# Plain fp32 products beside the transpositions, their remainders later on VectorE, and one GpSimd multiply ahead of a normalization, in a fused decoder layer

## What is computed

```python
q  = x + x @ Wq + bq;  ks = x + x @ Wk[k] + bk[k];  vs = x + x @ Wv[k] + bv[k]     # k = 0, 1
states = einsum('kbhnd,kbhne->kbhde', ks / 32, vs / 32)                            # per head, 16 x 16
state  = states[0] * states[1]
x1 = layernorm(x + (layernorm(q @ state) * ln_g + ln_b) @ Wo + bo)
sim  = (x1 @ Wqx.T) . (ctx @ Wk.T) * 64 ** -0.5                                    # 16 heads, 64 keys
attn = softmax(sim);  x2 = layernorm(x1 + (attn . (ctx @ Wv.T)) @ Wout.T + b_out)
```

## Time and profile before

| | |
|---|---|
| median of 3 runs | 1239.56 us (1238.46 to 1239.6) |
| the profiled execution | 1244.09 us, span 1242.4 us |
| mean granted TensorE clock | 0.99 of full speed |
| busy over the span | PE 97%, PE weight loads 85%, VectorE 69%, GpSimd 47%, ScalarE 45% |
| one iteration of the attention | about 48.5 us, 16 of them from about 112 us to 890 us |

### The profile page before, as it was taken

One profiled execution on the slowest core, in us unless ns is written; L12 is line 12 of the kernel. 1 busy time (PEld: TensorE's weight loads), 2 busy tenths in 40 slices (PEclk: granted clock), 3 DMA queues, 4 the chain that ended last, 5 costly groups with the idle time before them and its releaser, 6 DMA issues.

```text
span 1242.4 us, 27256 instructions
## 1 busy us (share of the span) xinstructions
PE 1203.1 (97%) x10512; PEld 1051.2 (85%) x10512; DVE 863.1 (69%) x1694; ACT 555.1 (45%) x1097; POOL 585.8 (47%) x968
## 2 busy tenths in 40 slices
PE   8987999999999999999999999989999999999998
PEld 7866888888888888888888888877799899899888
DVE  5545988889889889889898898988523423432435
ACT  2124556555555555465555555545523412421420
POOL 2223665666666666656666565655322112202201
PEclk9988999999999999999999999999999999999999
DMA  9821011021111011110211111310211022021001
GB/s 274 222 65 35 12 59 54 26 60 45 35 52 53 26 61 36 43 61 19 61 44 36 52 53 35 115 50 26 95 69 69 1 69 69 1 69 69 1 1 35
DMA packets 88739, 70.07 MB, mean 56 GB/s; under 512 B 41378, under 2 KB 82083, under 8 KB 88612
## 3 DMA queue, kind: packets, MB, share of 16 engines
q1 hardware_dynamic: 86580, 67.67, 18.0%
q10 hardware_dynamic: 2032, 0.66, 0.2%
HBM read 42.09 MB, written 26.22 MB: 55 GB/s over the span
## 4 chain that ended last, share of the span: by engine, by line
PE 71%; DVE 8%; issue 7%; POOL 6%; ACT 1%; POOLq 0%; DVEq 0%
PE sim L137 6%; PE sim L138 6%; PE sim L139 6%; PE ob L137 5%; PE ob L138 5%; PE ob L139 5%; PE pt L497 4%; PE pw L391 3%; PE pt L139 2%; PE pt L138 2%; PE pt L137 2%; PE pw L137 2%; PE pw L454 2%; PE pw L138 2%; PE pw L139 2%
## 5 line engine op out<-in xcount | busy, mean ns | idle before, releaser
L1619 POOL TENSOR_TENSOR w_lo<-w_raw,w_hi 128x2048 fp32r<-128x2048 f32 x16 | 73.8, 4614 | 220.9 <-ACT w_hi L1559 167.8
L137 PE MATMUL ob<-b_hi,pT_hi 128*128 128x256 f32 x512 | 151.0, 295 | 0.5 <-DVE pT_lo L879 0.5
L138 PE MATMUL ob<-b_lo,pT_hi 128*128 128x256 f32 x512 | 143.6, 280 | 0.0
L139 PE MATMUL ob<-b_hi,pT_lo 128*128 128x256 f32 x512 | 143.6, 280 | 0.0
L968 POOL TENSOR_TENSOR prob<-prob,rz 128x512 f32<-128x512 f32 x128 | 131.1, 1046 | 12.6 <-DVE rz L816 12.6
L732 ACT ACTIVATE pT_hi<-pt 128x512 fp32r<-128x512 f32 x128 | 76.2, 595 | 111.2 <-PE pt L497 110.6
L726 ACT ACTIVATE prob<-prob 128x512 f32<-128x512 f32 x128 | 81.1, 633 | 99.1 <-DVE prob L872 99.0
L137 PEld LDWEIGHTS ob<-b_hi,pT_hi 128*128 128x128 f32 x512 | 96.9, 189 | 9.0 <-issue 5.4
L138 PEld LDWEIGHTS ob<-b_lo,pT_hi 128*128 128x128 f32 x512 | 97.1, 190 | 1.9
L139 PEld LDWEIGHTS ob<-b_hi,pT_lo 128*128 128x128 f32 x512 | 96.3, 188 | 0.0
L867 DVE TENSOR_REDUCE mx<-sim 128x8 f32<-128x512 f32 x128 | 87.8, 686 | 6.6 <-PE sim L139 4.4
(11 more groups left out here) (244 smaller groups left out, 3726.5 us busy)
## 6 DMA issues: line engine op xcount, KB each, us to landing
xraw<-in_x SPq DMA_DIRECT2D x16, 512.0 KB, 4.0
kv_scratch<-stage SPq DMA_DIRECT2D x32, 256.0 KB, 3.6
x_scratch<-x SPq DMA_DIRECT2D x64, 128.0 KB, 1.7
out_x<-o_sb SPq DMA_DIRECT2D x64, 128.0 KB, 1.7
w_raw<-in_L_ffn_experts_inter SPq DMA_DIRECT2D x8, 1024.0 KB, 5.1
w_raw<-in_L_ffn_experts_out SPq DMA_DIRECT2D x8, 1024.0 KB, 7.8
kraw<-kv_scratch SPq DMA_DIRECT2D x16, 256.0 KB, 2.9
vraw<-kv_scratch SPq DMA_DIRECT2D x16, 256.0 KB, 2.8
```

The lines of the kernel that those rows point to most:

```text
L137: pe.matmul(out, lh, rh, start=first, stop=False)
L138: pe.matmul(out, lh, rl, start=False, stop=False)
L139: return pe.matmul(out, ll, rh, start=False, stop=last)
```

## The change

Three kinds of edit:

- `ORDER`: `B0`/`B1` move on TensorE from between the halves of `ob` in slot 0 to the end of the slot, in front of the next slot's transposes, on ScalarE to the start of slot 1 and on VectorE behind the sum and statistics there. `B2`/`B3` move in slot 1 from between the score halves to behind them, in front of the second transposes, with ScalarE and VectorE following later in the slot (VectorE behind the second shift). `A1`/`A3` move in slot 2 from between the halves of `ob` to the end of the slot; ScalarE and VectorE do them in slot 3, VectorE one at the very start and one behind the sum and statistics. `ST` moves in slot 3 on TensorE behind the second score half, and on VectorE from behind the first shift to behind the second.
- `pool_p`: the multiply of one half of the probabilities by `rz` becomes a function.
- `pool_slot`: in slot 2 the multiply of the first half stands ahead of `rstd` of the first norm; in all other slots the order stays.

```diff
     ORDER = {
-        "B0": ((0, 7), (0, 8), (1, 0)), "B1": ((0, 7), (0, 8), (1, 0)),
-        "B2": ((1, 1), (1, 1), (1, 3)), "B3": ((1, 1), (1, 1), (1, 3)),
+        "B0": ((0, 8), (1, 0), (1, 1)), "B1": ((0, 8), (1, 0), (1, 1)),
+        "B2": ((1, 2), (1, 3), (1, 5)), "B3": ((1, 2), (1, 3), (1, 5)),
...
-        "A1": ((2, 7), (2, 8), (2, 10)), "A3": ((2, 7), (2, 8), (2, 10)),
-        "ST": ((3, 1), (3, 1), (3, 3)),
+        "A1": ((2, 8), (3, 0), (3, 0)), "A3": ((2, 8), (3, 0), (3, 1)),
+        "ST": ((3, 2), (3, 1), (3, 5)),
...
+    def pool_p(pool, q, h):
+
+        part = by_head(prob[:, q, h * HK:(h + 1) * HK])
+        pool.tensor_tensor(part, part, rz[:, q, h * 8:h * 8 + 8].unsqueeze(2).broadcast_to([P, 8, NKV]),
+                           ALU.mult).then_inc(s["p_ready"], 1)
+
...
+        if has_sim and slot == 2:
+            need(pool, "rz_made", n + 1)
+            pool_p(pool, q, 0)
         if has_z and it != -1:
             pool_rstd(pool, 0, n + 4, q)
         if has_sim:
             need(pool, "rz_made", n + 1)
-            for h in range(2):
-                part = by_head(prob[:, q, h * HK:(h + 1) * HK])
-                pool.tensor_tensor(part, part, rz[:, q, h * 8:h * 8 + 8].unsqueeze(2).broadcast_to([P, 8, NKV]),
-                                   ALU.mult).then_inc(s["p_ready"], 1)
+            if slot != 2:
+                pool_p(pool, q, 0)
+            pool_p(pool, q, 1)
         if has_z and it != -1:
             pool_rstd(pool, 1, n + 4, q)
```

## The result

The changed kernel takes 1267.48 us (median of 4 runs, 1265.22 to 1268.38) against 1239.58 us (4 runs), a ratio of 1.0218 with a 95% interval of 1.0205 to 1.0231: slower by 27.9 us. 1266.6 us was forecast. Its profiled execution has a span of 1265.2 us.

The account below looks back on a forecast made before the run. Slot 3 was taken as bound by a chain from ST through GpSimd, ScalarE and VectorE to the queries. 14 iterations x 1.9 = 26.6 us, +0.5 without ST, -0.1 last batch: +27.0, so 1239.6 becomes 1266.6, range 1257 to 1280.

Parts of the forecast that it names:

- TensorE's switches: Each moved block saves about 0.05 us on TensorE; B0/B1 and B2/B3 together 0.10 an iteration, A1/A3 and ST where TensorE waits.
- The B remainders: In slot 1 on ScalarE and VectorE, the same operations in another order, costed at nothing; at most 1.2 us.
- GpSimd's multiply and rstd: Slot 2: first multiply 1.3 us sooner, TensorE's 0.45 wait gone; rstd ends near 534.8 instead of 534.3, VectorE idle some 0.9.
- VectorE's order: Slots 2 and 3: pT_lo 0.6 us later, ST 1.9 later behind the second shift; VectorE's own work reaches zw_lo unchanged.
- What queues behind it: Slot 3: GpSimd's state, nmr, ScalarE's norms, zw_hi, zw_lo and the queries all come 1.9 us later behind the late ST.
- TensorE's two waits: Slot 3: TensorE stands about 1.2 us before SB and 1.5 (elsewhere 1.7) before the queries.
- The rule by occupancy: A skill rule to optimize the busiest engine: TensorE's savings alone would count and time would fall; slot 3 speaks against it.
- The last but one iteration: The iteration without ST: VectorE's +0.6 us meets a bound softmax chain, forecast to cost +0.5 us.
- the last one: The last batch's iteration: the B moves were forecast to gain 0.1 us.
- The clock: Rival, 9%: slot 3's new waits lower the granted clock, up to 22 us more, 1289; in a third of iterations 1274.
- The second rival: 5%: TensorE's stream decides, sprod reached by 540.2 as before, 0.65 us gained an iteration, about -9 us, 1230.
- The third, no change: 3%: VectorE's own work reaches zw_lo at the same time and ScalarE's norms do not wait for nmr: 1239 us.

Follow-up runs that it names:

- only_b: The kernel before with only the ORDER rows of B0 to B3 from the change: 1237.56 us, iterations of 48.46 us, ratio 0.9979.
- only_pool: The kernel before with only GpSimd's first multiply of slot 2 put ahead of rstd: 1240.1 us, iterations of 48.54 us, ratio 1.0006.
- state_late: The changed kernel with GpSimd's state multiplies called in slot 3 behind the last norm's factors and the x1 bias: 1243.39 us, ratio 1.0025.
- st_early: The changed kernel with ST's operations on VectorE back behind the first shift: 1250.42 us, iterations of 49.16 us, ratio 1.0078.
- only_state_late: The kernel before with only GpSimd's state multiplies called in slot 3 behind the last norm's factors: 1240.55 us, ratio 1.0003.
- only_st: The kernel before with only ST's row of the change: 1260.97 us, iterations of 49.84 us, ratio 1.0176.
- state_late_old_rstd: As state_late, with GpSimd's rstd ahead of the first multiply in slot 2 again: 1237.94 us, iterations of 48.35 us, ratio 0.9975.
- state_late_a_undone: The changed kernel with A1/A3 as before and GpSimd's state multiplies moved as in state_late: 1232.41 us, iterations of 48.09 us, ratio 0.9945.
- state_late_only_b: As state_late_a_undone, but with ST's row as in the kernel before: 1236.3 us, iterations of 48.45 us, ratio 0.9983.

## Why the prediction was right

**TensorE's switches.** Right: `B0`/`B1` and `B2`/`B3` save 0.09 an iteration together (`only_b`), 0.10 was taken. The B remainders were costed at nothing, and nothing shows, as `only_b` has the whole gain. What a switch is made of stays open: the products of L454 and L443 run on quarters of the array (64*64 in their rows), so the kind of operand and the tiling change together. From a transposition to fp32r products, both on the whole array, the first step of `sim` takes 0.32 us instead of 0.23 (544.78 to 545.10, then 545.33), so part of the price needs no change of tiling. The 0.05 taken for `A1`/`A3` and for `ST` was not measured alone.

**GpSimd's multiply and rstd.** Right in both directions. The first multiply starts 0.09 us behind the end of `rz`, the transposition of slot 3 no longer waits, and VectorE stands 1.03 us for `rstd`, where 0.9 was reckoned. Alone, the reordering is worth nothing (`only_pool`).

**VectorE's order.** `pT_lo` was to come 0.6 later and `ST` 1.9. Counted from the start of slot 2, `pT_lo` comes at 13.76 instead of 13.07, 0.7 later, which is 0.6 with the slot's earlier start of nearly 0.1; `ST` 2.04, or 1.96. VectorE's own work was to reach `zw_lo` where it did: it is through 1.80 us before 556.66, at 545.2 on the old time axis, against 545.14.

**What queues behind it.** The step on which all hung. `state_late` takes nothing away but this queue, and `st_early` nothing but the maximum and shift in front of `ST`; they return 24 and 17 of the 28 us, and VectorE's amount of work, the same in all three, cannot explain either. The prediction gives TensorE's two waits as about 1.2 us, and 1.7 in its rivals or 1.5 among its signs; they are 0.96 and 1.40 of idle time, or 1.1 and 1.55 by the distance of the starts less the 0.12 of a matmul. On the old time axis the state was to be ready at 543.3 and the queries at 547.5; both hold within 0.1.

**The rule by occupancy.** The Trainium skill, Perfetto Trace Analysis, section Identifying the Most-Contended Engine, would have picked TensorE here too. Over the whole it is the busiest, but the change shortened slots 0 to 2 by 0.6 us together (34.75 us against 35.36) and the time rose; so the trace disagrees with reading the sum from TensorE's share. The Trainium skill, Perfetto Trace Analysis, section Optimization Strategy, says to find the gaps on that engine and the semaphore that each waits for. The trace agrees with this one: the two gaps of slot 3, now 0.96 and 1.40 us, name the chain.

**The sum.** Thirteen whole iterations grew by 1.91 us each, 24.8 together, and the three slots of the first one that are seen behind its start by 2.1: 26.9 us, where 26.6 was forecast for fourteen. Behind them two small terms were mis-sized. The last but one iteration, which has no `ST`, was underrated: its slots 2 and 3 take 22.49 us in `st_early`, which has the same order there, against 21.55 before, +0.94 instead of +0.5. In the last one the gain was underrated: its four slots take 39.83 us instead of 40.54, 0.7 less, where the B moves were given 0.1; `only_b` has the same shorter slot 1 (9.66 instead of 10.61) and longer slot 2 (11.05 instead of 10.72). That the two errors nearly cancel is luck. In the profiled execution of the change a fall of the clock, shown in the last section, adds another 1.56 us in slot 2 of the last but one iteration. With 0.07 saved in that iteration's first two slots, all that makes 28.6 us from slot 1 of the first batch to the end of the last slot (779.26 us against 750.65), and 27.1 without that fall, where 27.0 was forecast. The spans differ by only 22.8, because the setup took 5.8 us less in the one execution than in the other, and the medians by 27.9, which carry that scatter too.

**The rivals.** The clock did not fall inside the iterations: the granted clock is 1.00 in all four slots, and 1.00 from 140 to 809 us, in spite of the two waits. The second rival, a gain, asked for `sprod` by 540.2; on the old time axis it came at 542.1. The third, no change, asked that ScalarE's norms did not wait for `nmr`; they waited 3.05 us. `state_late` is the change with that condition made true, and it is 0.23 us an iteration over the kernel before, which is TensorE's wait in front of `SB`, less what it gains elsewhere.

## What to carry to other kernels

A wait belongs to the instruction's engine, not to the work it is for: before moving a producer later, look at which engine waits for it and list everything that stands behind that wait in its program. Here four operations of 0.7 us moved by 1.3 us held up a norm, a split and the queries on three other engines. Where two chains arrive at the same place together, shortening one alone gives nothing (`only_state_late`, 0.00 us), and lengthening it costs nearly in full (`only_st`, 1.29 of 1.33). Here a gain beyond the 0.09 of `B0` to `B3` came only when GpSimd's queue was out of the way and `ST` came late on VectorE, where it fills a wait: 48.35 in `state_late_old_rstd`, 48.09 in the fastest version.

## What the runs showed of the hardware

The scatter between profiled executions is not in the fourteen iterations with a state. They repeat within 0.2 us in every kernel, and what follows the last slot takes 367.6 us in all twelve traces. What differs is the setup and the last two iterations, both with the granted clock. These are windows of the kernel before and of `only_st` (the granted clock is the third number from the end):

```profile
60.00:90.00 30.00, 24.12 (x175) 20.23 (x174) 15.01 (x28) 7.01 (x15) 5.74 (x20) 0.90 0.31 81
90.00:120.00 30.00, 23.72 (x209) 19.50 (x209) 13.70 (x32) 9.70 (x22) 11.82 (x22) 0.76 0.10 36
```

```profile
60.00:90.00 30.00, 24.11 (x188) 20.23 (x187) 15.51 (x30) 7.13 (x16) 7.26 (x24) 1.00 0.31 79
90.00:120.00 30.00, 22.45 (x257) 17.51 (x256) 20.52 (x43) 15.46 (x35) 16.95 (x30) 1.00 0.11 37
```

The setup's program is the same in both. In the first execution the first batch's slot 1 began at 124.16 us, in the second, which kept the full clock, at 115.41, 8.75 us sooner. Over the twelve kernels the two go together: with a mean granted clock of 1.00 up to that slot it begins at 115.4, with 0.99 at 116.7, with 0.97 at 118.3 and 119.1 (the first is the change), with 0.94 at 121.8, with 0.92 at 123.7 to 124.2. So `only_st`'s profiled execution took 1252.1 us, 8.9 under its median, and a comparison of two spans (1250.4 and 1242.4) would have called its cost 8 us, where the medians say 21. In the changed kernel slot 2 of the last but one iteration lay partly in such a spell (slots 2 and 3):

```profile
833.73:845.52 11.79, 11.79 (x180) 10.31 (x180) 8.66 (x17) 5.17 (x10) 6.09 (x13) 0.86 0.16 24
845.52:857.78 12.26, 8.28 (x60) 7.19 (x53) 10.19 (x22) 6.13 (x11) 6.88 (x15) 1.00 0.07 23
```

The same slot at full clock takes 10.23 us in `st_early`: 1.56 us for one fall, behind a wait of 2.19 us in front of the slot. The length of the wait alone does not decide it. All twelve traces have a wait of 2.19 to 2.28 us at this place. The clock in the slot behind it fell to 0.86 or 0.87 in five of them (the change, `only_pool`, `state_late_old_rstd`, `state_late_a_undone`, `state_late_only_b`) and stayed at 1.00 in seven, the kernel before and `st_early` (2.20 us) among them. In front of the last iteration nine waits of 2.59 to 3.00 us brought a fall, and three of 2.54, 2.60 and 2.85 (`only_st`, `only_b`, `state_late_old_rstd`) brought none. The waits of 0.96 and 1.40 us in the iterations with a state never did. What decides between the longer ones was not tried.
